# The state's update as two 256-column products, products that fill a wait of TensorE, and three moves in hand-written orders

## What is computed

```python
x = u + layernorm(mamba(layernorm(u)))
out = x + layernorm(ffn(layernorm(x)))
```

```python
S = S * exp(dt * A) + dt * outer(x, B)      # per head
y = S @ C + D_param * x
y = (y * silu(z)) @ W_out.T
```

## Time and profile before

| | |
|---|---|
| median of three runs | 1364.97 us (1364.5 to 1366.99) |
| the profiled execution, its own time | 1367.52 us |
| its span, first to last instruction | 1365.8 us |
| TensorE busy | 1308.9 us, 96% of the span, 6720 products |
| VectorE, ScalarE, GpSimd busy | 938.3 us (69%), 554.6 us (41%), 491.3 us (36%) |
| mean granted TensorE clock | 0.987 of full speed |

### The profile page before, as it was taken

How to read it: one execution, slowest core, us unless ns; L and a number is a source line. 1 busy time by engine, 2 the same in 40 slices (tenths; PEclk the granted TensorE clock), 3 DMA queues, 4 the chain that set the end, 5 groups by cost and what they waited for, 6 DMA issues and landing times. The chain is left out here.

```text
span 1365.8 us, 18801 instructions
## 1 busy us (share of the span) xinstructions
PE 1308.9 (96%) x6720; PEld 640.2 (47%) x6720; DVE 938.3 (69%) x1889; ACT 554.6 (41%) x1042; POOL 491.3 (36%) x701
## 2 busy tenths in 40 slices
PE   4899989998999999999999999999999999999997
PEld 2444545554444444444444444444444445444443
DVE  7888869996597657865787568766886565644332
ACT  5666767885434234433333233424342222132120
POOL 1322232233334643453543533354435344401102
PEclk9889999999999999999999999999999999999999
DMA  5045336424301422133211330233114102301201
GB/s 173 17 106 140 82 80 138 105 65 111 85 24 45 118 62 55 31 85 89 74 32 44 96 86 24 62 101 89 28 31 109 54 24 62 93 32 39 70 0 54
DMA packets 132812, 96.16 MB, mean 70 GB/s; under 512 B 102000, under 2 KB 102000, under 8 KB 132720
## 3 DMA queue, kind: packets, MB, share of 16 engines
q1 hardware_dynamic: 124752, 78.74, 22.5%
q10 hardware_dynamic: 7968, 16.23, 4.6%
HBM read 54.05 MB, written 16.78 MB: 52 GB/s over the span
## 5 line engine op out<-in xcount | busy, mean ns | idle before, releaser
L1513 PE MATMUL bank<-fxt,ffn_hi 128*128 128x512 f16 (+1 forms) x1408 | 418.9, 379 | 7.8 <-DVE gact L1898 6.3
L1513 PE MATMUL bank<-fxt,ffn_lo 128*128 128x512 f16 (+1 forms) x704 | 266.8, 379 | 0.0
L1513 PEld LDWEIGHTS bank<-fxt,ffn_hi 128*128 128x128 f16 (+1 forms) x1408 | 139.6, 100 | 177.7 <-DVE gact L1898 9.3
L1527 PE MATMUL bank<-ffn_hi,h_hi 128*128 128x512 f16 (+1 forms) x352 | 133.5, 379 | 0.0
L1527 PE MATMUL bank<-ffn_hi,h_lo 128*128 128x512 f16 (+1 forms) x352 | 133.4, 379 | 0.0
L1527 PE MATMUL bank<-ffn_lo,h_hi 128*128 128x512 f16 (+1 forms) x352 | 133.3, 379 | 0.0
L1407 PE MATMUL bank<-mask,diag 128*128 128x416 f16 x640 | 120.4, 343 | 6.4 <-ACT ffn_lo L956 4.5
L656 POOL TENSOR_TENSOR state<-state,ex 64x512 f32<-64x512 f32 x32 | 36.1, 1129 | 233.3 <-PE bank L1470 232.1
L1008 ACT ACTIVATE gact<-bank,c_gate_half 128x512 f32<-128x512 f32 (+1 forms) x88 | 60.0, 682 | 145.8 <-PE bank L1513 144.0
L1898 DVE SCALAR_TENSOR_TENSOR gact<-gact,bank 128x512 f32<-128x512 f32 (+1 forms) x88 | 60.3, 685 | 85.6 <-ACT gact L1008 84.7
L1771 DVE SCALAR_TENSOR_TENSOR xs<-cin,conv_w_sb,xs 128x512 f32<-128x512 f32 x114 | 103.5, 907 | 20.6 <-ACT xs L897 17.6
(11 more groups left out here) (195 smaller groups left out, 2240.2 us busy)
## 6 DMA issues: line engine op xcount, KB each, us to landing
codes_sb<-codes ACTq DMA_DIRECT2D x76, 208.0 KB, 3.4
ures<-u SPq DMA_DIRECT2D x32, 256.0 KB, 3.0
x_scratch<-x SPq DMA_DIRECT2D x32, 256.0 KB, 2.4
ut<-x_scratch SPq DMA_DIRECT2D x16, 512.0 KB, 4.3
xres<-x_scratch SPq DMA_DIRECT2D x32, 256.0 KB, 3.1
out<-dn SPq DMA_DIRECT2D x32, 256.0 KB, 2.0
ut<-u SPq DMA_DIRECT2D x15, 512.0 KB, 4.4
ffn_hi<-w_in_t SPq DMA_DIRECT2D x4, 580.0 KB, 8.6
```

What stands on the lines that cost most here:

```text
L1513: last = nc.tensor.matmul(bank, wt[:, c0:c0 + w], fxt[:, :, half, k, :], start=(k == 0 and n == 0), stop=(k == KC - 1 and n == 2))
L1527: last = nc.tensor.matmul(banks[FFN_BANKS[turn % 3]][:], h[0:w, m, tok], wt[0:w, d0:d0 + D], start=(m == 0 and n == 0), stop=(m == MB - 1 ...
```

## The change

The update of the state is issued as two products of 256 columns, the first into partitions 0 to 63 of `tok_bank`, the second into partitions 64 to 127, and the addition to the state as two additions of 256 columns. Twelve products of 512 columns, whose result nobody reads, are issued between `project_z(0, 3)` and `prepare_x(0, 0)`; they write `carried_bank` and first wait for `decays(0, 0)`. VectorE's `ln_stats("u", 1, 0)` moves from behind `conv(0, 2)` to behind `conv_silu(0, 3)`. In SyncE's order `transpose_y(0, 3)` and `residual(0, 3)` change places. GpSimd waits for the end of its own `add_residual` in tiles 0 and 1 before it goes on.

```diff
@@ SyncE, tile 0 @@
                 store_x1(0, 1)
+
+                transpose_y(0, 3)
                 residual(0, 3)
-
-                transpose_y(0, 3)
                 store_x1(0, 2)
@@ GpSimd, add_residual @@
                     x1_ready.inc(nc.gpsimd.tensor_tensor(x1[:], x1[:], ures[:], ALU.add))
+                    if t < LAG:
+                        pool.wait_ge(x1_ready.sem, x1_ready.now(t, c + 1))
@@ TensorE @@
+                def keep_busy(n):
+
+                    pe.wait_ge(decay_ready.sem, decay_ready.now(0, 2))
+                    for _ in range(n):
+                        nc.tensor.matmul(carried_bank[:], ident_h[:], win_hi[:, 0, 0:D], start=True, stop=True)
@@ TensorE, scan @@
-                    s_done.inc(nc.tensor.matmul(tok_bank[h, :], bt, xtok[:], start=True, stop=True))
+                    for g in range(2):
+                        last = nc.tensor.matmul(tok_bank[g * NST:(g + 1) * NST, 0:D // 2], bt,
+                                                xtok[:, g * (D // 2):(g + 1) * (D // 2)], start=True, stop=True)
+                    s_done.inc(last)
@@ TensorE, order @@
                 project_z(0, 3)
+                keep_busy(12)
                 prepare_x(0, 0)
@@ VectorE, y_sum @@
-                    state_ready.inc(nc.vector.tensor_tensor(state[to, :], state[h, :], tok_bank[h, :], ALU.add))
+                    for g in range(2):
+                        cols = slice(g * (D // 2), (g + 1) * (D // 2))
+                        last = nc.vector.tensor_tensor(state[to, cols], state[h, cols],
+                                                       tok_bank[g * NST:(g + 1) * NST, 0:D // 2], ALU.add)
+                    state_ready.inc(last)
@@ VectorE, order @@
                 conv(0, 2)
-                ln_stats("u", 1, 0)
                 conv_silu(0, 1)
                 conv(0, 3)
                 conv_silu(0, 2)
                 conv_silu(0, 3)
+                ln_stats("u", 1, 0)
                 z_gate(0, 1)
```

## The result

The changed kernel takes 1352.39 us (median of 4 runs, 1352.29 to 1353.32), beside 1365.37 for the kernel before on the same chip (4 runs, 1364.5 to 1366.99): 13.0 us faster, ratio 0.9906 [0.989, 0.9922]. The forecast of 1350.0 is 2.4 us from the time, inside the range.

What follows compares the result with a forecast made beforehand. TensorE was taken as the bound from 420 to 1160 us, with costly waits and half-clock stretches earlier. 5.0 + 4.9 + 5.1 = 15.0 us, from the median 1364.97 to 1350.0; range 1344 to 1359.

Steps and rivals of the forecast that it cites:

- A: Ahead of the first scan: twelve products and moved ln_stats shorten TensorE's wait and hold its clock; 5.0 us.
- B: End of tile 0: SyncE's transpose ahead of residual removes a 3.51 us wait and the slow clock behind; 4.9 us.
- C: State update as two products in different array halves: partial overlap saves 0.16 us an update, 5.1 us over 32.
- GpSimd's own wait: In eight places it delays GpSimd's next instruction by some 0.1 us; counted as nothing.
- products still start in order: State update: only the first half's second pass and the second half's first overlap; 0.21 us before the load's cost.
- the end that I had at -0.43: Favourable extreme for the state update: all four passes overlap two by two, saving 0.43 us an update.
- The second assumption: State update: the second half's weight load, issued one product ahead at most, costs 0.05 us of the overlap.
- the sign that I had named: Line 1486: second and third starts closer than 0.2 us, 0.85 us to the next instruction; 1.0 would refute.
- Rival 1: State update: the halves don't overlap, so only the other two terms' 9.9 us remain, 1355.1 us; chance 0.27.
- rival 3: Line 1486: each change of half costs, 1.7 us instead of 1.01, total 1377; chance 0.04, plus 0.03 for a single drain.
- I expect the clock to stay at 2.4 GHz there: First scan, from 56.73 us: with TensorE idle 1.0 us instead of 5.23, the clock would not drop.
- Rival 2: First scan: the clock falls all the same, leaving 0.2 to 2 us of that term, 1353 to 1355; chance 0.16.

Runs made afterwards that it cites:

- Part C added alone: The kernel before with only the update as two 256-column products and two additions: 1356.72 us, 12.0 us faster than before.
- uneven: The changed kernel with the update cut at column 384, 384 columns to the first half and 128 to the second: 1354.72 us in its one run.
- same_half: The changed kernel with both 256-column products in the same 64 partitions and one addition of 512 columns: 1363.94 us, ratio 0.997 to the kernel before.
- inner_halves: The changed kernel with line 1488's inner products also cut into two 64-token products, one per half of the partitions: 1328.88 us, ratio 0.9714 to the kernel before.
- codes_late: The changed kernel with ScalarE's codes_to_half(6), which issues a load of codes, moved behind two slices of u: 1350.94 us, ratio 0.9882 to the kernel before.

## Why the prediction was right, and where it wasn't

The time came out right, and each of the three terms was off; the errors had different signs. Against 5.0 (A), 4.9 (B) and 5.1 (C) stand 2.1, 3.4 and 10.2, each taken out of the changed kernel. That is 15.7, beside the 13 to 15 of the whole. (Part C added alone gave 12.0.) That the sum met the time to 2.4 us is luck: with A and B as forecast and the 12.0 of part C it would have been 1343.1, outside the range, whose fast end allowed 0.28 us an update. GpSimd's own wait, which I had put at nothing, was never taken out alone, so its price isn't shown.

**Part C.** The mechanism was right, two halves overlap, and the size was 2 to 2.4 times too small in time: 0.42 us an update instead of 0.16, 10.2 to 12.0 us instead of 5.1. The step that failed is "products still start in order, so only the second pass of the first half and the first of the second can overlap". They don't start in order across halves (uneven), and all four overlap two by two, the end that I had at -0.43. The second assumption, that a load lies open for 0.05 us, failed as well: both halves' loads start 5 to 7 ns apart. So the sign that I had named, a second and a third start less than 0.2 us apart and 0.85 us to the next instruction, did not come: in order of time those two starts are 260 ns apart, and the next instruction is there at 0.585. Rival 1, no overlap, is refuted by 585 ns against the 1010 of same_half; rival 3, a price for each change of half, has the wrong sign. Here the rule that I had weighed against the change is out a second time. The Trainium skill, TensorE: Matmul & The Clock Gate, The mechanism, says that weight loads overlap with products under way only when the row groups differ, and that products are in program order in start and end; in these kernels the rows are the same, the loads overlap, and a later product's second pass starts 207 ns ahead of an earlier one's. The order of the ends isn't refuted: the semaphore of the last product is counted up behind the longer half (890 ns in uneven). The rule of the Trainium skill, TensorEngine Tiling (Array Packing), Key Properties, that tiles load and multiply independently, is what the traces agree with.

**Part A.** On TensorE all steps up to line 1488 were right within 0.2 us: `prepare_x` at 58.28 (58.37 forecast), the twelve products 2.76 us (2.6), line 1488 released by VectorE at 62.52 (62.55). GpSimd's `weigh_x` ended at 63.8, not at 64.6, and does not set the time of the update (65.32). Two steps failed. "I expect the clock to stay at 2.4 GHz there" held from 56.7 to 63.38 only, 0.86 us behind the end of the wait of 1.45 us for VectorE; from there TensorE ran for 10.24 us at 1.2 GHz. Line 1488 took 2.80 us to the next (1.83 at full clock, 3.45 before), line 1495 1.12 in its record (0.65), and the decode behind it was slow. I had left 2 to 3 us for this and had put the likely value above it. So the second scan was 3.6 us earlier, not 5.8. And in the trace read first the lead did not last: the step that the prediction did not have is the transpose of u at 85.66, which was issued 3.6 us earlier and landed only 0.5 us earlier. I had followed the lead as far as the second scan and entered it whole in the sum; that holds only where the next wait is for the engine that was sped up. By the end of the run 2.1 us are left of it, not clear of zero. Rival 2 (A at 0.2 to 2) is thus close to what happened to part A, by a way half its own.

**Part B.** The path was as forecast: the transpose issued right behind `y_split`, at 180.09; the wait of 3.51 us gone; the slow stretch behind it gone; VectorE's wait 2.87 us instead of 7.88. In the trace it gives the 5.2 us of that place less one update's 0.42, 4.8 us, for which the forecast said 4.9. Undone, it costs 3.4 us by the medians. What takes the rest behind that place stays open.

**The addition.** A pair ends 0.16 us later, between the 0 and 0.3 that the earlier trace rows allowed, and I took 0.1. In tile 0 TensorE's wait for the state rose from 0.77 to 0.95 us.

## What to carry to other kernels

A TensorE product whose output has 64 rows uses half of the array: split its columns over the two halves of the partitions, as evenly as they go, and the update takes the time of one half (1005 to 585 ns here). The same holds for products with 128 output rows and few columns, which are bound by their weight loads: split the output rows, although that doubles the instructions. Both pay only where TensorE is the bound. A lead that is won ahead of a DMA is a gain only if that DMA lands earlier too; before it is entered in a sum, look at what else moves while the transfer is under way, and follow the lead to the end of the run.

## What the runs showed of the hardware

- The two halves of TensorE's array (output partitions 0 to 63 and 64 to 127) each run their own loads and passes in order and do not wait for each other; an update of 256 float32 columns in each, their passes starting 6 to 8 ns apart, takes 585 ns to the next instruction, and 1010 with both in one half (same_half).
- With 384 columns in one half and 128 in the other, the semaphore of the second product, whose last pass starts at 166 ns, is counted up at 890 ns, behind the longer half (uneven).
- A pass of a float32 product with 128 columns of weights and 64 columns of data starts every 112 ns; as two halves a pair of passes starts every 58 (inner_halves).
- Where a product with 128 output rows is followed by one with 64, the last pass took 204 ns to the next start, in a stream of 112; where both had 64, 51 ns in a stream of 58.
- A DMA transpose of the same size took 5.5 us to landing where the loads of codes came behind it, and 8.7 to 12.3 in the traces of the changed kernel, with those loads beside it. The runs of that kernel spread over 10 us (1347.23 to 1357.65); that the transpose is the reason isn't shown, and codes_late, without the loads beside it, spreads over 8 us (1348.57 to 1356.99).
